# Constant products from the start, batch 0's columns on ScalarE's queue, and the sort's products between two halves of the value-output ones

## The reference, cut to what matters

```python
# 1. attention with one score matrix for all 16 heads: the heads' factors are all ones
qf = x @ Wq.T; kf = x @ Wk.T                 # rank 64
attn = softmax(einsum('hr,bir,bjr->bhij', ones, qf, kf))
out = einsum('bhij,bhjd->bhid', attn, (x @ Wv.T) split in heads) @ Wo.T
x = layernorm(x + out)
# 2. four experts from ctx, chosen by token id
expert = minimum(clip(ids, 0, 12499) // 3125, 3)
y = silu(x @ ctx[expert].T) * (x @ ctx[expert].T) @ ctx[expert].T
x = layernorm(x + y)
# 3. four experts, the best one by a router (softmax of x @ Wr + br), its output times its probability
x = layernorm(x + top_w * (silu(x @ Wg[e]) * (x @ Wu[e]) @ Wd[e]))
```

## Time and profile before

| what | us |
|---|---|
| median of 3 runs | 195.75 |
| the runs | 195.70, 195.75, 196.77 |
| the profiled execution, its own time | 194.93 |
| its span | 192.6 |
| TensorE busy | 173.3 (90%) |
| VectorE busy | 129.4 (67%) |
| ScalarE busy | 102.7 (53%) |
| GpSimd busy | 103.2 (54%) |

### The profile page before, as it was taken

One profiled execution on the slowest core, in us unless ns is written; L12 is line 12 of the kernel. 1 busy time (PEld: TensorE's weight loads), 2 busy tenths in 40 slices (PEclk: granted clock), 3 DMA queues, 4 the chain that ended last, 5 costly groups with the idle time before them and its releaser, 6 DMA issues.

```text
span 192.6 us, 3906 instructions
## 1 busy us (share of the span) xinstructions
PE 173.3 (90%) x972; PEld 139.3 (72%) x972; DVE 129.4 (67%) x406; ACT 102.7 (53%) x273; POOL 103.2 (54%) x131
## 2 busy tenths in 40 slices
PE   1999998799999799989999999999999999999810
PEld 0777767457888546668888788888888888888610
DVE  3267879768687878536654454444799977888950
ACT  3137687535577655547664956534555423455530
POOL 7000268653927676528772368850688800377783
PEclk9999999999999999999999999999999999999985
DMA  5999999348998223247544005554050000011010
GB/s 147 357 344 417 376 362 347 104 140 213 344 353 342 88 66 87 69 109 208 190 162 159 9 0 167 173 166 158 0 167 0 0 0 3 0 58 56 22 63 24
DMA packets 15605, 29.14 MB, mean 151 GB/s; under 512 B 1758, under 2 KB 12000, under 8 KB 15458
## 3 DMA queue, kind: packets, MB, share of 16 engines
q1 hardware_dynamic: 13856, 25.68, 40.2%
q0 software_dynamic: 1440, 3.22, 4.7%
q10 hardware_dynamic: 290, 0.01, 0.1%
HBM read 20.41 MB, written 9.28 MB: 154 GB/s over the span
## 4 chain that ended last, share of the span: by engine, by line
PE 68%; POOL 12%; issue 8%; DVE 5%; DMA 3%; POOLq 1%; ACT 1%; DVEq 0%; ACTq 0%
PE bank L506 14%; PE bank L508 14%; PE bank L507 13%; POOL out_tokens L495 5%; PE bank L762 4%; POOL rstd L422 3%; PE bank L683 3%; PE bank L660 3%; PE bank L586 3%; PE bank L520 2%; PE bank L595 2%; PE bank L514 2%; DMA x_sorted<-buf,slot 2%; PE bank L533 2%; PE bank L617 1%
## 5 line engine op out<-in xcount | busy, mean ns | idle before, releaser
L418 POOL TENSOR_TENSOR w_lo<-stage,w_hi 128x512 fp32r<-128x512 f32 x40 | 51.3, 1305 | 34.5 <-ACT w_hi L839 29.7
L960 ACT ACTIVATE gate<-bank 128x256 f32<-128x256 f32 x44 | 17.0, 386 | 48.1 <-PE bank L508 46.8
L1262 DVE TENSOR_TENSOR hid<-bank,gate 128x256 f32<-128x256 f32 x44 | 18.7, 424 | 30.4 <-ACT gate L960 30.1
L506 PE MATMUL bank<-w_hi,xr 128*128 x88 | 35.8, 407 | 1.4 <-DVE xr L1215 0.8
L508 PE MATMUL bank<-w_hi,xr 128*128 x88 | 34.7, 394 | 0.0
L507 PE MATMUL bank<-w_lo,xr 128*128 x88 | 34.7, 394 | 0.0
L506 PE MATMUL bank<-w_hi,hT 128*128 x88 | 28.5, 324 | 0.7 <-DVE hT L1267 0.7
L422 POOL TENSOR_TENSOR rstd<-mv,mhalf 128x1 f32<-128x1 f32 x19 | 11.3, 597 | 31.6 <-DVE mv L1101 31.3
L839 ACT ACTIVATE w_hi<-stage 128x512 fp32r<-128x512 f32 x45 | 27.0, 631 | 0.3 <-PE bank L508 0.3
L508 PE MATMUL bank<-w_hi,hT 128*128 x88 | 24.8, 282 | 0.0
L507 PE MATMUL bank<-w_lo,hT 128*128 x88 | 24.8, 281 | 0.0
(11 more groups left out here) (189 smaller groups left out, 325.9 us busy)
## 6 DMA issues: line engine op xcount, KB each, us to landing
stage<-in_w_ffn SPq DMA_DIRECT2D x15, 768.0 KB, 4.8
rows<-x_sorted SPq DMA_DIRECT2D x22, 132.0 KB, 2.3
x_sorted<-padrow SPq DMA_DIRECT2D x1, 2244.0 KB
x_sorted<-padrow SPq DMA_DIRECT2D x1, 2112.0 KB
buf<-in_x_tok SPq DMA_DIRECT2D x1, 1024.0 KB, 11.4
w_hi<-in_ctx SPq DMA_DIRECT2D x1, 1024.0 KB, 11.6
w_hi<-in_ctxT SPq DMA_DIRECT2D x1, 1024.0 KB
x_sorted<-padrow SPq DMA_DIRECT2D x1, 792.0 KB, 13.1
```

Of the source, the lines that this page charges most:

```text
L418: g.tensor_tensor(out=lo, in0=src, in1=hi.bitcast(F32), op=ALU.subtract).then_inc(split_lo, 1)
L506: mm(dst, xhi, whi, start=start, stop=False)
L960: a(gate[:, (T + j) % 2, :], fA[j % 2][:, 0:FQ], ACT.Silu).then_inc(silu_done, 1)
L1262: v.tensor_tensor(out=hid[:, (T + j) % 2, :], in0=fA[j % 2][:, FQ:2 * FQ], in1=gate[:, (T + j) % 2, :], op=ALU.mult).then_inc(h_done, 1)
```

## The change

GpSimd writes `ones` first, with a semaphore of its own, and TensorE starts seven constant products as soon as it is there, where it ran two after all constants. The wait for the constants and the router's three products move to the place behind `qk_of(0)`. Batch 0's columns are loaded by ScalarE's queue, ahead of the ids; SP's queue no longer issues them. The product of the value and output weights is cut into two halves, with the sort's four products between them. TensorE takes `scores(0)` ahead of `z_of(0)`. ScalarE, no longer VectorE, copies `wvo` out, and it does `exps(0)` ahead of `copy_z(0)`, of the first two splits and of `copy_qk(1)`. VectorE does `maxes(1)` behind all tables of the sort.

```diff
-        CONSTS = 24
+        CONSTS = 23
...
             sp.dma_start(awt[:, 0:QKW], aw[:, 0:QKW]).then_inc(d_aqk, 16)
-            sp.dma_start(xT[:, :, 0:SEQ], xT_rows[:, :, 0:SEQ]).then_inc(d_xT0, 16)
             sp.dma_start(awt[:, QKW:], aw[:, QKW:]).then_inc(d_avo, 16)
...
+            g.memset(ones[:], 1.0).then_inc(ones_ready, 1)
             const(g.memset(padrow[:], 0.0))
             const(g.memset(ident[:], 1.0))
             const(g.memset(below[:], 1.0))
-            const(g.memset(ones[:], 1.0))
...
-            pe.wait_ge(consts, CONSTS)
-            idle_products(2)
+            pe.wait_ge(ones_ready, 1)
+            idle_products(7)
             pe.wait_ge(d_aqk, 16)
             pe.wait_ge(d_xT0, 16)
             qk_of(0)
 
-            pe.wait_ge(d_avo, 16)
-            for d in range(DK):
+            pe.wait_ge(consts, CONSTS)
+            pe.wait_ge(d_wr, 32)
+            for k in range(DK):
+                mm(pWrSum, ones_f[:], wr[:, k, :], start=k == 0, stop=k == DK - 1)
+            mm(pBr, one_row[:], br[:], start=True, stop=True).then_inc(br_done, 1)
+
+            def wvo_half(d):
                 for k in range(DK):
                     last = mm(pW[:, d * D:(d + 1) * D], wv[:, k, d * P:(d + 1) * P], woT[:, k, :],
                               start=k == 0, stop=k == DK - 1)
-            last.then_inc(wvo_done, 1)
-
-            pe.wait_ge(consts, CONSTS)
+                return last
+
+            pe.wait_ge(d_avo, 16)
+            wvo_half(0)
             pe.wait_ge(m1_ready, CHUNKS)
...
             mm(pR1[:, 72:72 + E], ones[:], m1cum[:, 2 * SORTED, :], start=True, stop=True).then_inc(r1_done, 1)
-
-
-            pe.wait_ge(d_wr, 32)
-            for k in range(DK):
-                mm(pWrSum, ones_f[:], wr[:, k, :], start=k == 0, stop=k == DK - 1)
-            mm(pBr, one_row[:], br[:], start=True, stop=True).then_inc(br_done, 1)
+            wvo_half(1).then_inc(wvo_done, 1)
...
+            scores(0)
             z_of(0)
-            scores(0)
...
+            act.dma_start(xT[:, :, 0:SEQ], xT_in.rearrange("p (k n) -> p k n", k=DK)[:, :, 0:SEQ]).then_inc(d_xT0, 16)
             act.dma_start(ids[:], ids_in).then_inc(d_ids, 16)
...
             copy_qk(0)
+            act.wait_ge(wvo_done, 1)
+            a(wvo.rearrange("p k n -> p (k n)"), pW[:, :], ACT.Copy).then_inc(wvo_copied, 1)
+            exps(0)
             copy_z(0)
             splits(ACT_SPLITS[0])
             copy_qk(1)
-            exps(0)
             copy_z(1)
...
-            dve.wait_ge(wvo_done, 1)
-            v.tensor_copy(wvo.rearrange("p k n -> p (k n)"), pW[:, :]).then_inc(wvo_copied, 1)
-
...
-            maxes(1)
-
...
             v.tensor_tensor(out=slot1[:], in0=key1[:], in1=moved[:], op=ALU.add).then_inc(route1, 1)
+            maxes(1)
```

More of the change, by code:

```diff
@@ L209, in route_kernel @@
         pad_ready = sem("pad_ready")
+        ones_ready = sem("ones_ready")
         wvo_done, wvo_copied = sem("wvo_done"), sem("wvo_copied")
```

## The result

The changed kernel took 199.74 us (198.12, 198.62, 200.86 and 201.13) against 195.72 before: ratio 1.016, interval 1.011 to 1.021 (the run of 201.13 is left out of it; with it the medians are 2.1% apart). The interval lies wholly above 1, so it is slower, where 193.55 was forecast; three executions carry the 1.6%. The profiled execution took 198.12 with a span of 196.2, 3.6 more than before.

A forecast was written before the change was run, and what follows sets the result against it. TensorE, busy for 90% of the span, was taken to bound the kernel. An earlier start of 2.3 us less 0.1 for late chunks gave 195.75 - 2.2 = 193.55 us, within a range of 192.8 to 195.2.

The forecast's parts named there:

- the 5.7 that I took: Start of the kernel: the clock rises at 5.7 us, 4.6 after TensorE's first product, so `qk_of(0)` ends at 6.0.
- The maxima behind the tables: VectorE, `maxes(1)` behind the sort's tables: ready at 16.0 against 18.40 before, with no loss.
- The second chunk of expert weights: Later stage 1: lands near 19.4, wanted at 18.1; ScalarE stands 1.3 us (0 to 2.3), taken in by later idle time.
- The columns' row: Batch 0's columns on ScalarE's queue: land at 4.5 us (3.9 to 6.97), near the row of the same load, 3.4 before.
- The rival on late loads: Loads share and come late: with ids at 6.0, `qk_of(1)` starts 1.2 us earlier; middle 194.6, chance 0.20.
- The wait that followed was the router's: Router's products moved behind `qk_of(0)`: loads land at about 5.5, products cost nothing until about 6.8.
- if the clock again rises 4.6 us after the first product: `qk_of(0)`: with the clock up at 5.7, four instructions take about 1.5 us, until 6.0 (7.03 before).
- `qk_of(1)` as forecast (11.55): TensorE after batch 0: `qk_of(1)` starts at 11.55 against 13.83 before, 2.3 us earlier.
- The rival on the clock (not lifted earlier): Constant products fail to lift the clock, low until 9 us: `qk_of(1)` at 12.8, 1.0 off, 194.7; chance 0.08.
- A chain of events without a fixed hour: Start of the later stages: no fixed hour, so a gain that lives through stage 1 should reach the end.
- the sum: Whole kernel: 2.3 us gained at `qk_of(1)` less 0.1 for late chunks of expert weights, 2.2 us off.

The follow-up runs named there:

- early_dense: early_only with nine early constant products instead of seven and two more behind `qk_of(0)`; 195.67 us, ratio 0.998 to the kernel before.
- early_only: Kernel before with only `ones` written first and seven constant products from 1.1 us, instead of two at 4.3; 195.75 us, ratio 0.999.
- bridged: Changed kernel, loads still late, with 17 constant products instead of 7 ahead of `qk_of(0)` and 6 behind it; 196.30 us, ratio 1.004 to the kernel before.
- queue_only: Kernel before with only batch 0's columns moved to ScalarE's queue, ahead of the ids; 196.68 us, ratio 1.004.
- loads_back: Changed kernel with batch 0's columns issued second on SP's queue again; 196.95 us, ratio 1.003 to the kernel before.
- filled: loads_back with nine constant products instead of seven, two behind `qk_of(0)`, router's products between the weights' first half and the sort's; 195.29 us, ratio 0.995 to kernel before.
- filled_again: The kernel called filled, run once more unchanged; 194.82 us, ratio 0.994 to the kernel before.
- order_only: loads_back with two constant products behind all constants instead of seven early; ratio 1.003 to the kernel before by seven executions, median of all twelve 197.44 us.
- router_mid: order_only with the router's products between the weights' first half and the sort's; ratio 1.000 to the kernel before by six executions, median of all 197.32 us.
- before_less_pad: Kernel before with the first padding write into the second scratch tensor cut from 16 to 11 of 33 blocks, the rest moved to the second write; ratio 1.001.
- both_back: Changed kernel with columns on SP's queue and the router's products behind the value-output product again; 196.23 us, ratio 1.003 to the kernel before.
- router_back: Changed kernel with the router's three products and their wait back behind the value-output product; 196.59 us, ratio 1.004 to the kernel before.

## Why the prediction was wrong

**Right.** TensorE starts at 1.06 and the seven products end at 4.05. The value weights' product waits for nothing but its order. The maxima behind the tables cost nothing. The constant products did lift the clock, even before the 5.7 that I took. The second chunk of expert weights was not late in the changed kernel: ScalarE did not wait for it. Where it was wanted earliest, ScalarE waited for 0.18 us (early_dense, at 18.86) and 0.28 (early_only, at 19.71), less than the 1.3 of the prediction. What follows `qk_of(1)` in attention moved with it (last scatter 2.91 later for 2.94 at `qk_of(1)`).

**The columns and what stands behind them.** I took 4.5 for the columns, 4.7 for the ids and 5.5 for the router's loads. They landed at 5.8, 6.1 and 7.9. The columns' row was the wrong neighbour: 3.4 us was the time of a load with only 128 KB ahead of it in its queue, and here 640 KB and more of the other queue were under way beside it. The rival on late loads had this and the right middle for the ids (6.0), but priced the ids alone. The wait that followed was the router's, of which the prediction said that it costs nothing until 6.8; nothing stood for what happens past that hour. In the changed kernel it is 1.0 us, behind columns that put `qk_of(0)` off by 1.4 against the forecast (5.94 for 4.5). Lateness by itself is worth about 0.4% in time (bridged, queue_only).

**The clock.** This is the step that failed by most. It was "if the clock again rises 4.6 us after the first product" and then nothing more: once up it was taken to stay up through gaps of 1.9 and 1.0 us. It fell at 7.2 and stayed down until 14.0. The prices at both levels were in the earlier trace rows; the case in which it falls again was not on the list. bridged shows its size: 3.0 us on the work up to `qk_of(1)`, 1.2% in time. Together the terms close: columns 1.4, router's wait 1.0, low clock 3.0, less 0.4 for a `qk_of(0)` that ran at full speed, make 5.0 of the 5.2 us between `qk_of(1)` as forecast (11.55) and as measured (16.77). The rival on the clock (not lifted earlier) is what loads_back shows, and at 194.7 it was too cheap: it had the clock up at 9, while it came at 13.

**The carry.** "A chain of events without a fixed hour" was wrong too, though it did not decide the changed kernel, which carried its 2.9 us of delay to stage 2 whole. A lead is not carried like that. In early_dense 1.8 us of it were 0.2 when the first sorted rows were read; in filled 1.2 at the last scatter were 0.4 at the first tile. In these profiles the sixth scatter started within about a us of the padding's end and took 4.0 and 3.3 us, where 2.4 is its time before. That the padding is the reason was argued from the hour and not shown. The hour could have been read in the profile: the GB/s of the slices stay near 350 until 34 us, and the sixth scatter started 1.7 us behind that. I looked for such hours among the expert weights only. It is not the only loss. In filled_again the first tile started 1.0 us earlier than before, the third root of stage 2 still 0.9 and the fourth 0.3, and the span is shorter by only 0.2. So of the 1.1% that the sum said, filled and filled_again give 0.5 to 0.6%: about half of the lead was never made at `qk_of(1)`, and what was made got lost in part on the way.

**Open.** Why the executions of the new order (order_only, router_mid) fall into two groups some 3 us apart. The one profile of an upper group, order_only's, has the clock low until 17. Nine of these eleven executions have a mean granted clock of 0.983 to 0.988, as high as the faster ones; a late first rise would not show in it (the last list tells why), so it fits, but is not shown. Why the clock stayed low that long in loads_back and order_only. Where the 0.7 us near 66 in the changed kernel's profile comes from. Between the third and the fourth root of stage 2 the kernel before took 6.9 us and filled too, the changed kernel 7.6 and most of the other profiles 7.4 to 7.5, early_only and filled_again with them, so it is not this change alone; in filled_again it takes 0.6 of the lead, and VectorE stands for the same "remote" wait there.

## What to carry to other kernels

Constant products at the start are worth having only if they reach the real work: a gap behind them can undo the clock for longer than they lifted it, so count them by when the data land at the latest, and fill the later gaps too. A load that is moved takes its followers along, and a product moved ahead of its old neighbours brings its wait: for each wait on the new path write down what happens if the load is two us late. Before a gain is carried to the end, look for transfers that end shortly before the next stage begins, and for waits in the later stages that do not move with it; either can be an hour that the gain does not pass. And since the same start came out 0.8 us apart in two profiles, a gain of that size needs more than one.

## What the runs showed of the hardware

- A 256 KB load issued 0.45 us earlier on a second queue landed at 4.8, 5.3, 5.8 and 6.2 in four profiles, on the first queue at 4.65 before and at 4.5 to 5.3 in the others. The loads of the first queue, which had one less ahead of them, gained: the value weights landed at 5.9 to 6.1 instead of 6.9, x by rows at 13.0 to 13.6 instead of 15.2. The ids, now behind the moved load in the second queue, landed at 6.1 to 6.4, not at 3.2. The Trainium skill (DMA: Bandwidth & Descriptors, Issuing engines are not separate DMA queues) says that loads issued by different engines run on the same 16 DMA engines and interleave; these numbers agree.
- In the kernels whose first product is at 4.3 us the clock rose at 7.3 (before_less_pad), by 8.75 (router_mid), near 9 (before), 10.8 (queue_only, with TensorE idle for 1.0 us from 5.3) or 17 (order_only). With products from 1.06 it rose at 3.7 to 6.8, in both_back at 8.4 and in loads_back at 13.2.
- The column of the granted clock reads 1.00 up to the first change that was recorded, also where the durations show half speed (L520 at 5.33 in the earlier trace rows). At the start of a kernel the clock is read off the durations.
- After waits the clock fell: at 7.2 with TensorE idle for 1.9 and then 1.0 us (changed kernel), at 11.3 behind idle times of 1.3 and 1.4 (router_back), at 41.4 behind one of 1.7 (early_dense). It came back at 14.0, 14.7 and 44.8.
- An indirect scatter of 128 rows landed in 2.4 us with little else moving, and in 2.5 to 4.3 when it was started at 33.9 to 35.4 us, about the end of a 2.1 MB write.
